# Side work of an attention loop in single products, and five tiles of values moved into its first unit

## The reference, cut to what matters

```python
x = x + _L0_xattn_ref(_layernorm(x), ctx_1024, ctx_1024, mask, wq, bq, wk, bk, wv, bv, wo, bo)
x = x + _L0_ffn_ref(_layernorm(x), ...)      # 2 shared experts, top 2 of 8 routed ones
x = x + _L1_xattn_ref(_layernorm(x), ctx_1024, ctx_1024, mask, Wq, bq, Wk, bk, Wv, bv, Wo, bo)
x = x + _L1_ffn_ref(_layernorm(x), ...)      # sqrt((x cos(theta))**2 + (x sin(phi))**2)

# one attention
q, k, v = (split_heads(t) for t in (q_in @ Wq + bq, k_in @ Wk + bk, v_in @ Wv + bv))
score = einsum('bhqd,bhkd->bhqk', q, k) / sqrt(16) + mask
out = einsum('bhqk,bhkd->bhqd', softmax(score), v) @ Wo + bo
```

## Time and profile before

| | us |
|---|---|
| median of three runs | 1262.23 |
| the profiled execution | 1261.12 |
| its span, first to last instruction | 1259.4 |
| PE busy | 1164.9 (92%) |
| ACT busy | 1015.5 (81%) |
| DVE busy | 720.3 (57%) |
| POOL busy | 168.5 (13%) |
| the 800 exponentials of line 925, 1061 ns each | 748.4 |
| the value products of line 1834 | 436.0 |
| mean granted clock of PE | 0.997 |

### The profile page before, as it was taken

How to read it: one execution, slowest core, us unless ns; L and a number is a source line. 1 busy time by engine, 2 the same in 40 slices (tenths; PEclk the granted TensorE clock), 3 DMA queues, 4 the chain that set the end, 5 groups by cost and what they waited for, 6 DMA issues and landing times. The chain is left out here.

```text
span 1259.4 us, 43578 instructions
## 1 busy us (share of the span) xinstructions
PE 1164.9 (92%) x17850; PEld 581.9 (46%) x17850; DVE 720.3 (57%) x1697; ACT 1015.5 (81%) x1484; POOL 168.5 (13%) x204
## 2 busy tenths in 40 slices
PE   8888899899898999999999999988889999999897
PEld 5422232232222356667999998752222233232233
DVE  5325777767746577554666666662545444443447
ACT  3599999999999854443566666639999999999994
POOL 5111111011001030333000011032321000000000
PEclk9999999999999999999999999999999999999999
DMA  6235853643645333221343355133120010010002
GB/s 196 65 118 193 272 169 104 197 151 107 205 155 177 103 119 113 86 71 51 117 123 116 116 141 160 44 99 96 49 58 24 11 38 2 11 38 2 2 3 67
DMA packets 106305, 124.94 MB, mean 99 GB/s; under 512 B 25091, under 2 KB 89310, under 8 KB 106142
## 3 DMA queue, kind: packets, MB, share of 16 engines
q1 hardware_dynamic: 89088, 85.95, 22.1%
q0 software_dynamic: 9328, 29.37, 7.4%
q10 hardware_dynamic: 7726, 7.26, 1.9%
HBM read 70.27 MB, written 46.95 MB: 93 GB/s over the span
## 5 line engine op out<-in xcount | busy, mean ns | idle before, releaser
L925 ACT ACTIVATE prob<-banks 128x1024 f32<-128x1024 f32 x800 | 748.4, 1061 | 7.3 <-PE banks L1799 3.8
L1834 PE MATMUL banks<-prob,v 64*32 64x512 f32 x6400 | 436.0, 592 | 0.0
L1799 PE MATMUL banks<-zone,kst 52*32 52x512 f16 x6144 | 316.4, 383 | 65.7 <-ACT prob L925 58.2
L1799 PEld LDWEIGHTS banks<-zone,kst 52*32 52x32 f16 x6144 | 86.7, 89 | 444.0 <-ACT prob L925 429.5
L1834 PEld LDWEIGHTS banks<-prob,v 64*32 64x32 f32 x6400 | 117.4, 106 | 24.1 <-issue 2.2
L2503 PE MATMUL banks<-xsT_d,w 128*128 128x128 f16 x1776 | 123.6, 219 | 2.7 <-DMA w<-weight_parts 1.5
L2503 PEld LDWEIGHTS banks<-xsT_d,w 128*128 128x128 f16 x1776 | 108.6, 98 | 11.8 <-issue 8.8
L2514 PE MATMUL banks<-w,hh 128*128 128x256 f16 x592 | 107.0, 273 | 0.0
L2300 DVE TENSOR_TENSOR hl<-hid,hh 128x128 f16<-128x128 f32 x296 | 83.2, 291 | 30.9 <-ACT hh L2227 23.2
L2223 ACT ACTIVATE hid<-banks,b 128x128 f32<-128x128 f32 x222 | 74.5, 369 | 25.0 <-PE banks L2503 21.2
L2466 PE MATMUL banks<-w,hh 128*128 128x256 f16 x480 | 79.0, 273 | 2.1 <-DVE outb_d L2385 2.1
(11 more groups left out here) (302 smaller groups left out, 1367.2 us busy)
## 6 DMA issues: line engine op xcount, KB each, us to landing
weight_parts<-late SPq DMA_DIRECT2D x54, 256.0 KB, 3.9
w<-weight_parts POOLq DMA_DIRECT2D x24, 512.0 KB, 3.9
late<-in_L_ffn_W_r SPq DMA_DIRECT2D x43, 256.0 KB, 4.4
weight_parts<-more SPq DMA_DIRECT2D x26, 256.0 KB, 3.6
zone<-q_parts SPq DMA_DIRECT2D x180, 32.0 KB
slot_rows<-late POOLq DMA_DIRECT2D x14, 384.0 KB
more<-in_L_ffn_W_r SPq DMA_DIRECT2D x21, 256.0 KB, 4.2
xs_d<-slot_rows ACTq DMA_DIRECT2D x39, 128.0 KB, 2.1
```

The source lines that it names most:

```text
L925: nc.scalar.activation(prob[:, t % P_RING, 2 * (n % 2):2 * (n % 2) + 2, :], score[G % S_RING], ACT.Exp, scale=0.25).then_inc(exp_done, 1)
L1799: last = nc.tensor.matmul(score[G % S_RING][j:j + GROUP, a, :], kst[stack, 2 * q + n % 2, t * P + j:t * P + j + GROUP], qst[stack, u % Q_R ...
L1834: last = nc.tensor.matmul(outp[u % 2][GROUP * j:GROUP * (j + 1), a, :], v[rows, t, u % NQ, j, :], prob[rows, (u * KT + t) % P_RING, j if t ...
```

## The change

It has four parts.

1. **Five value tiles later.** In both layers tiles 8 to 12 are not projected before the loop but in unit 0, at tiles 0, 2, 4, 6 and 8 (`project_later`), into the same two banks, and DVE copies them out (`later_values`) ahead of everything else that it has in unit 0. The loop waits for eight value tiles instead of 13; `outputs` of tiles 8 to 12 and the "last" scores of unit 0 wait for the later ones. The value weights must outlive the first exponentials: in layer 0 they are loaded into `more`, in layer 1 POOL copies them into `late`, ahead of its first reciprocal root, and PE and ACT wait for that copy.
2. **Early queries in layer 1.** Only bounds (1, 0) and (1, 1) and value tile 7 stand ahead of the query products, which come before bounds (1, 2) and (1, 3). DVE makes the low part of the turned tokens ahead of the product of bound (1, 1).
3. **Single products.** Query and wave pieces are one product each, turn pieces two transposes, a logit piece one tile of four. `plan` spreads each kind over a range of tiles; several atoms can fall in one tile.
4. **Other tiles.** Queries in layer 0 now end at tile 7 instead of 4; in layer 1 the first query of q = 1 ends at tile 12 instead of 10, and the first wave of q = 2 takes tiles 10 to 12 instead of 10 and 11. The output products stand on neighbouring tiles (6 to 9, 2 to 5). The other three waves of q = 3 take tiles 2 to 10, two products a tile. "last" moves with them.

```diff
-V_BETWEEN = 9
+V_BETWEEN = 8
+V_LATER = 5
+LATER_AT = (0, 2, 4, 6, 8)
-LAST_AT = ((4, 11, 10, 8), (5, 8, 5, 11))
-FIRST_LAST_AT = ((8, 11, 10, 8), (5, 11, 10, 6))
-SIDES_AT = [((6, 7, 9, 10), (2, 3, 5, 6, 8, 9), (2, 4, 6, 8), (2, 4, 6)),
-            ((2, 4, 6, 7, 9, 10), (2, 4, 5, 7, 9, 10), (2, 4, 6, 8, 10, 11), (2, 4, 5, 7, 8, 10))]
-LATE_AT = ((), (7, 9), (2, 4, 6, 8), ())
+LAST_AT = ((4, 11, 11, 10), (5, 6, 6, 11))
+FIRST_LAST_AT = ((11, 11, 10, 8), (11, 11, 10, 6))
+
+SIDE_PRODUCTS = DH * 3
...
-        jobs = keys + queries + bounds if first else keys + bounds + queries
+        ahead_of_queries = len(BCH) + 2
+        jobs = keys + queries + bounds if first else keys + bounds[:ahead_of_queries] + queries + bounds[ahead_of_queries:]
...
+                pool.wait_ge(g.pre_loaded, PRE_LOADS)
+                nc.gpsimd.tensor_copy(wv, wv_early).then_inc(wv_copied, 1)
...
-                for n in range(2):
-                    bound_product(1, n)
+                bound_product(1, 0)
                 low_turned()
-                for n in range(2, len(BCH)):
-                    bound_product(1, n)
-                for name in queries:
+                bound_product(1, 1)
+                for n, name in enumerate(queries):
                     low_part(*name)
+                    bound_product(1, 2 + n)
                 largest(1)
...
+            def later_values(n):
+
+                t = KT - V_LATER + n
+                if n == 0:
+                    dve.wait_ge(v_cleared, 2)
+                dve.wait_ge(later_projected, n + 1)
+                for b in range(2):
+                    src = project[n % 2][:, 0:D].rearrange("p (i b j r) -> p b i j r", i=2, b=2, j=QH)[:, b]
+                    dst = v[:, t, :, :, :].rearrange("p (i b) j n -> p b i j n", b=2)[:, b, :, :, HD * b:HD * (b + 1)]
+                    ins = nc.vector.tensor_copy(dst, src)
+                    if b:
+                        ins.then_inc(later_ready, 1)
...
+                if u == 0:
+                    for n in range(V_LATER):
+                        later_values(n)
...
+            def project_later(n):
+                if n == 0 and not first:
+                    pe.wait_ge(wv_copied, 1)
+                if n >= 2:
+                    pe.wait_ge(later_ready, n - 1)
+                value_products(project[n % 2], KT - V_LATER + n, wv).then_inc(later_projected, 1)
...
+                if first and done:
+                    groups = (((outs[0], 6, 10),), ((outs[1], 2, 6), (turns, 6, 10)),
+                              ((asked[0], 2, 8), (back, 8, 11)), ((asked[1], 2, 8), (logit, 8, 10)))[q]
+                elif first:
+                    groups = ((), ((turns, 7, 11),), ((asked[0], 2, 8),), ((asked[1], 2, 8),))[q]
+                elif done:
+                    groups = (((turns, 2, 5), (outs[0], 6, 10)), ((outs[1], 2, 6), (asked[0], 7, 13)),
+                              ((asked[1], 2, 6), (back, 7, 9), (waves[0], 10, 13)), ((sum(waves[1:], []), 2, 11),))[q]
                 else:
+                    groups = ((), ((turns, 7, 11),), ((asked[0] + asked[1], 2, 10),), ())[q]
+                at_tile = {t: [] for t in range(KT)}
+                for atoms, t0, t1 in groups:
+                    for n, atom in enumerate(atoms):
+                        at_tile[t0 + n * (t1 - t0) // len(atoms)].append(atom)
...
+                    if u == 0 and t in LATER_AT:
+                        project_later(LATER_AT.index(t))
+                    for piece_of_work in pieces[t]:
+                        side(*piece_of_work)
```

More of the change, by code:

```diff
@@ L1679, in project_values @@
                     pe.wait_ge(v_ready, t - 1)
[L1680 to L1688, removed]
+                value_products(project[t % 2], t, wv_early).then_inc(v_projected, 1)
+            def project_later(n):
[4 more added lines that the diff above has]
+                value_products(project[n % 2], KT - V_LATER + n, wv).then_inc(later_projected, 1)
             def project_last_value():
@@ L1710, in first_products @@
                 project_last_value()
-                rest = range(V_MORE[layer], KT - V_LATE)
+                rest = range(V_MORE[layer], KT - V_LATER - V_LATE)
                 for i, (_, o, n) in enumerate(bounds):
@@ L1737, in later_products @@
                 turn_x()
[L1738 to L1742, removed]
+                bound(1, 1)
+                norm(half)
+                project_values(V_BEFORE)
                 pe.wait_ge(untangled, DH)
@@ L1746, in later_products @@
                     project_queries(o)
[L1747 to L1750, removed]
+                for n in range(2, half):
+                    bound(1, n)
+                    norm(half + n - 1)
+                norm(2 * half - 1)
             bound_matrix()
@@ L1903, in plan @@
                 ahead, done = c + 1 < NC, c >= 1
-                turns = [("turn", c + 1, 0), ("turn", c + 1, 1)] if ahead else []
-                outs = [("out", c - 1, i, n, k) for i in range(DH) for n in range(2) for k in range(DH)] if done else []
-                asked = [("query", c + 1, o, k) for o in range(DH) for k in range(DH)] if ahead else []
-                back = [("xturn", c - 1, 0), ("xturn", c - 1, 1)] if done else []
-                waves = [("wave", c - 1, i, h) for i in range(TPC) for h in range(DH)] if done and not first else []
@@ L1909, in plan @@
-                logit = [("logit", c - 1)] if done and first else []
-                if first:
-                    pieces = (outs[0:4], outs[4:8] + turns, asked[0:2] + back, asked[2:4] + logit)[q]
-                else:
-                    pieces = (turns + outs[0:4], outs[4:8] + asked[0:2], asked[2:4] + back + waves[0:2], waves[2:8])[q]
-                times = SIDES_AT[layer][q]
-                if not first and not done:
-                    pieces, times = ([], turns, asked, [])[q], LATE_AT[q]
-                elif not done or q == 0 or (q == 2 and not first):
-                    times = times[len(times) - len(pieces):]
@@ L1919, in plan @@
-                return {(LAST_AT if done else FIRST_LAST_AT)[layer][q]: ("last", c, q), **{t: piece for t, piece in zip(times, pieces)}}
+                pairs = range(TPC // 2)
+                turns = [("turn", c + 1, h, k) for h in range(DH) for k in pairs] if ahead else []
+                outs = [[("out", c - 1, i, n, k) for n in range(2) for k in range(DH)] if done else [] for i in range(DH)]
+                asked = [[("query", c + 1, o, k) for k in range(SIDE_PRODUCTS)] if ahead else [] for o in range(DH)]
```

109 lines of the change are left out of this document (71 added, 38 removed).

## The result

The changed kernel takes **1274.55 us**, the median of four runs (1271.53 to 1278.12), beside 1262.89 for the kernel before (four runs, 1260.45 to 1265.11): ratio 1.0092, 95% interval 1.0075 to 1.011. The forecast was 1264.8 with a range up to 1270.8, so the loss is 11.7 us where 2.6 to 3.7 was expected, and outside the range. The profiled execution of after took 1271.53, with a span of 1269.7 against 1259.4, at a mean granted clock of 0.991 against 0.997. It is the fastest of the four, so its rows explain 10.3 us, and 1.4 of the median's 11.7 lie outside them.

A forecast was written before the change was run, and what follows sets the result against it. ACT's exponentials were taken to bound both loops, with PE close behind. From 1261.1 us, layer 0's terms summed to +0.3 and layer 1's to +3.4, giving 1264.8 us, range 1257.0 to 1270.8.

The forecast's parts named there:

- What bounds the kernel, and the prices: Both loops: exponentials on ACT bound them; PE has 0.51 us a tile for side work, a lone product costs 0.43.
- the rival "a lone product costs 0.215": Both loops: a lone product costs 0.215 us, not 0.43, so spreading is free and the time is 1248; chance 0.04.
- Layer 0's start: Before layer 0's first score: five value tiles fewer bring the scores 2.8 us earlier (2.0 to 3.5).
- Layer 1's start: Before layer 1's first score: earlier queries, not the value tiles, bring the scores 1.5 us earlier (1.0 to 1.8).
- Five value tiles, and the clock: Unit 0: late value tiles cost 2.1 us in each layer; the clock's fall adds 0 in layer 0, 0.6 in layer 1.
- Single products: Side work spread over tiles in both loops: -0.8 us in layer 0, +1.2 (0.3 to 2.0) in layer 1.
- wait (a): Layer 0, q = 2 (units 6 and 10): later queries make DVE's last scores late, 0.75 twice, 1.5 us (0 to 3).
- wait (c): Layer 1, unit 7: DVE normalises before reading the finished banks, so PE waits 1.0 us (0.5 to 1.6).
- Who waits now: Three waits around DVE's order: 1.5 and 0.3 us in layer 0, 1.0 us in layer 1.
- (b): Layer 0, unit 0: five copies ahead of x's statistics make the last scores 0 to 0.6 late: 0.3 us.
- Slower by more: Layer 0: DVE's cuts run late in every unit with six or seven, five units losing 1.5: 1270.8 us; chance 0.12.
- same: Whole kernel: the measured time falls within 1256 to 1268.5 us, not told from no change; chance 0.74.

The follow-up runs named there:

- the filling: The changed kernel plus 8 (layer 0) and 12 (layer 1) products that nothing reads, in PE's idle time ahead of the first scores; 1271.82 us, ratio 1.0054.
- the run with three: The mixed kernel with layer 1's slow unit 6 mended and three value tiles late in layer 0 instead of five; 1260.17 us, ratio 0.9976.
- values back: The changed kernel with its five value tiles back ahead of the first score in both layers; 1270.86 us, ratio 1.0062.
- layer 0 alone: The changed kernel with the kernel before's side work, early queries kept, late values in layer 0 only; 1262.82 us, ratio 0.9996.
- the mixed kernel: The changed kernel with late values in layer 0 only, query products two to a tile, transpose pairs alone, outputs spaced, waves in threes; 1261.16 us, ratio 0.9982.

## Why the prediction was wrong, by its own steps

- **What bounds the kernel, and the prices.** Right. A lone product in the timeline of after, between score sets that start at 111.85 and 112.49:

```profile
111.85 0.39 PE L1827 MATMUL banks<-zone,kst 52*32 52x512 f16 x8
112.17 0.39 PE L1918 MATMUL banks<-xpT,wqp 128*128 128x512 f16 x1
112.49 0.41 PE L1827 MATMUL banks<-zone,kst 52*32 52x512 f16 x8
```

  From one score set to the next 0.64, less 0.22, is 0.42; 0.43 was said. The record of its weight load stands at 112.17 too, 0.32 behind the score set's start: it wasn't ahead of the product. Two waves in a tile took 0.87 - 0.22 = 0.65, 0.64 was said. A value tile, 867.03 to 868.43 in layer 1, took 1.40 - 0.22 = 1.18; 1.17 was said. So the rival "a lone product costs 0.215" is dead. The Trainium skill, "TensorE: Matmul & The Clock Gate", "Step-by-step: what each phase is for", has the next weights loaded during the matmul in flight, where the row groups don't conflict or the load goes to the background buffer; the measured 0.42 shows that between score sets and a full product this doesn't hide the change-over.
- **Layer 0's start.** -2.8 said, -3.0 measured.
- **Layer 1's start.** -1.5 said, -2.4 measured. The queries stood 1.5 earlier behind the turned tokens, as worked out (2.61 instead of 4.10 by starts). But I had the query loads land just when the scores start, and so "they aren't the price" of the four value tiles. They were most of it: the scores start 2.7 earlier behind the turned tokens, 1.2 more than the queries moved, and with five tiles back behind early queries the first exponential came 13.5 after the turned tokens, against 11.8 with late tiles and 14.2 before. Early queries alone gave 0.7 where 1.5 was said, and the tiles 1.7 where nothing was. The flags don't gate, as said: the scores waited for the query loads. POOL's copy of the weights took 0.77, with 4.70 of POOL's waiting still behind it, so it was free as said.
- **Five value tiles, and the clock.** +2.1 said for layer 0, +2.4 measured; +2.1 and +0.6 said for layer 1, +2.8 measured. Right in sum. In layer 1 the filling went with 0.5 less in unit 0, and 3.41 us of half clock where there had been 10.24. The Trainium skill, "TensorE: Matmul & The Clock Gate", part 1, says that activity releases the throttled state: the one profile with filling agrees in layer 1, with those figures, and shows no effect in layer 0, where 3.41 us of half clock remained behind later, thin work.
- **Single products.** Layer 0: -0.8 said for all, of which -0.6 for units 2 and 3; with 1.5 for wait (a) the other 13 units should have lost 1.3 and lost 0.5. Units with outputs rose by 0.25 to 0.29 in q = 0 (0.2 to 0.3 said) and by 0.1 in q = 1; units 6 and 10 fell by 0.19 and units 7 and 11 not at all (-0.04, +0.04), where 0.3 each was said. Layer 1, units 1 to 15: +2.2 said with wait (c), +2.2 measured, in part by luck, as wait (c) gave 0.4 less than was said. But **units 2 and 3 are the step that failed.** I took their old query pieces to stand at tiles 2 and 4, as in later chunks (so does the list under "The change", by which queries in layer 0 ended at tile 4), and so credited 0.3 each for spreading them and put the wait for the bank at nothing. The table's offset (`times[len(times) - len(pieces):]`, for units without finished work) puts them at 6 and 8, and 4 and 6. Spreading from tile 2 was a move four tiles forward, past DVE's late reading of unit 1. Said -0.6 for the two, measured +5.7 in the trace; moving unit 2's products back gave 5.3 of its 28.44 us back.
- **Who waits now.** (a), DVE's late last scores in q = 2, was said as 0.75 in units 6 and 10: the trace of after shows 23.15 and 23.19 in units 6 and 7, and 1.29 for one interval at the start of 7. DVE was late as said, but the dearer victim was the next unit's first query product, and its price in unit 7 is 0 in one execution, 1.5 to 1.8 in another. I had costed DVE's order at fixed durations, though rows 13 showed gaps that belong to DMAs. (b) nothing seen in after; with a value tile at tile 9, in the run with three, it cost 1.2. (c) said 1.0, on top of 0.2 for the waves; unit 7 rose by 0.9 in all. Units 11 and 15, with the same waves and no such wait, rose by 0.27 and 0.20, so the wait itself cost about 0.6, and PE stood for 0.53: the mechanism was right, its price too high by 0.4.
- **Sum and chances.** The trace's 10.3 is 6.6 over the forecast's 3.7: 6.3 for units 2 and 3, 2.2 between the layers (1.6 of it luck), less 0.9 at layer 1's start and 0.8 in layer 0's other units; what is left is under 0.3. The median's 11.7 may hold the waits that vary besides; no profile of a slower execution of this kernel shows it. Without the 6.3 the trace would have stood 4.1 over the kernel before, near the 3.7 of the forecast, but only with the 1.6 of luck in it. "Slower by more" named DVE's order, but in many units a little, not in one unit by 5; "same" got 0.74 and should have got less, since three waits were argued from margins under 1 us.

## What to carry over

When a table of places is replaced by a rule, list for every unit, old and new, the place of each piece beside the time at which its bank comes free; a piece that moves forward is an added wait until the trace shows its margin. Margins against an engine that waits for DMAs have to be read as a spread over executions, and one profile shows one draw of it. And when work is moved from a start into a loop that has no slack, count what the loop pays: here 3.0 was won and 2.4 lost in one layer, 2.4 and 2.8 in the other.

## What was not expected of the hardware

**The clock goes with a good part of the spread between executions.** Over 70 executions of the kernel before, the mean time falls with the mean granted clock, though not at every step: 1264.8 us at 0.991 (7 executions), 1263.9 at 0.992 (18), 1264.3 at 0.993 (11), 1262.4 at 0.995 (16), 1262.1 at 0.996 (12), 1259.8 at 0.997 (3). The kernel after ran at 0.989 to 0.992. The experts' stage, which no experiment touched, shows a half-clock stretch some 36 us behind layer 0's loop in five of the twelve profiles (466.08 in after, 468.99 with values back, 461.79 with layer 0 alone) and none at that place in the others, though PE waits 2.1 us just ahead of it in them too. In all five, the 3.41 us at half clock with PE full shifted what follows by 1.6 to 1.7 us.

**One stop that nothing in the trace explains.** In the mixed kernel PE stood for 2.12 us in unit 15 of layer 0, waiting for nothing that the profile shows, and the unit took 26.27 instead of 23.2:

```profile
417.67 0.40 PE L1849 MATMUL banks<-zone,kst 52*32 52x512 f16 x4
420.19 0.41 PE L1828 MATMUL banks<-zone,kst 52*32 52x512 f16 x8 [2.12 <-issue]
```

The scores before it were last scores of the same unit, and two kernels with the same plan there had no such stop. Behind it came 3.41 us of half clock (421.00 to 424.41), so the unit lost 3.0 us in all. Its cause stays open.
